# Two transformer layers on one core: the first attention item's operands copied chunk by chunk, and the zero rows copied before the second item's operands

## The reference, cut to what matters

```python
q = (x @ Wq + bq)...   # 16 heads of 16 values
k = (x @ Wk + bk)...   # 4 groups, each shared by 4 heads
v = (x @ Wv + bv)...
q_r = apply_rope(q / |q| * alpha * sqrt(16));  k_r = apply_rope(k / |k|)
attn = softmax(where(causal, q_r @ k_r.T / sqrt(16), -inf))
y = attn @ v;  x = layernorm(x + y @ Wo + bo)
```

## Time and profile before

| | |
|---|---|
| median of 3 runs | 808.29 us (807.83 to 812.68) |
| the profiled execution | 806.76 us |
| its span, first to last instruction | 805.1 us |
| busy, share of the span | TensorE 92%, VectorE 51%, ScalarE 49%, GpSimd 21% |
| mean granted TensorE clock | 0.952 of full |
| head of layer 0 | to about 88.6 us |
| first scores of layer 0 | 90.08 us |
| first scores of layer 1 | 383.01 us |

### The profile page before, as it was taken

How to read it: one execution, slowest core, us unless ns; L and a number is a source line. 1 busy time by engine, 2 the same in 40 slices (tenths; PEclk the granted TensorE clock), 3 DMA queues, 4 the chain that set the end, 5 groups by cost and what they waited for, 6 DMA issues and landing times.

```text
span 805.1 us, 10943 instructions
## 1 busy us (share of the span) xinstructions
PE 742.9 (92%) x3831; PEld 333.1 (41%) x3831; DVE 411.9 (51%) x998; ACT 394.4 (49%) x517; POOL 169.1 (21%) x185
## 2 busy tenths in 40 slices
PE   5999799999989899896999999989999999999996
PEld 1646222224322544342222222324466457448355
DVE  1579436334758788955043333365432842642524
ACT  1244688886868152553788888773121121130110
POOL 0012434343233123322143222331200200000000
PEclk9996599999999889999899999999999999999998
DMA  8401433332210000022444444470000000000000
GB/s 283 111 0 18 74 56 59 54 57 38 38 32 2 1 0 14 0 48 45 82 80 81 81 81 82 80 200 1 0 1 0 27 0 1 26 0 0 26 1 26
DMA packets 31601, 36.36 MB, mean 45 GB/s; under 512 B 7664, under 2 KB 19757, under 8 KB 31389
## 3 DMA queue, kind: packets, MB, share of 16 engines
q1 hardware_dynamic: 31541, 35.60, 21.8%
HBM read 12.74 MB, written 2.10 MB: 18 GB/s over the span
## 4 chain that ended last, share of the span: by engine, by line
PE 64%; DVE 15%; SPq 7%; ACT 6%; issue 4%; DMA 2%; POOL 1%; DVEq 0%; ACTq 0%; POOLq 0%
PE ps L1996 16%; PE ps L1255 13%; PE ps L1238 10%; PE ps L2020 9%; PE ps L1618 3%; SPq L972 3%; SPq L965 3%; ACT probs L1319 3%; PE ps L398 2%; DVE stats L289 1%; DVE raw L1155 1%; PE ps L643 1%; PE ps L667 1%; PE ps L1605 1%; PE ps L2006 1%
## 5 line engine op out<-in xcount | busy, mean ns | idle before, releaser
L1319 ACT ACTIVATE probs<-ps 128x1024 f32<-128x1024 f32 (+1 forms) x320 | 275.8, 965 | 66.2 <-PE ps L1238 65.9
L1238 PE MATMUL ps<-ops_mem 99*128 99x512 bf16 (+3 forms) x768 | 164.7, 336 | 14.6 <-issue 5.5
L1255 PE MATMUL ps<-probs,vstat 128*32 128x512 f32 (+3 forms) x1536 | 166.9, 507 | 11.4 <-DVE raw L1155 8.3
L1996 PE MATMUL ps<-ops_mem,parts_mem 128*128 128x512 f32 x320 | 147.2, 605 | 1.2 <-DVE probs L2048 1.2
L1335 POOL TENSOR_SCALAR_AFFINE_SELECT probs<-probs 128x512 f32<-128x512 f32 x128 | 85.0, 664 | 225.0 <-ACT probs L1319 224.3
L1238 PEld LDWEIGHTS ps<-ops_mem 99*128 99x128 bf16 x768 | 57.6, 99 | 164.2 <-ACT probs L1319 86.7
L1155 DVE COPY raw<-ps 128x512 f32<-128x512 f32 x32 | 22.1, 691 | 140.3 <-PE ps L1255 140.1
L1942 ACT ACTIVATE ops_mem<-ps 128x512 f32<-128x512 f32 x40 | 23.9, 597 | 142.7 <-PE ps L1996 139.9
L1996 PEld LDWEIGHTS ps<-ops_mem,parts_mem 128*128 128x128 f32 x320 | 58.9, 191 | 68.7 <-issue 66.0
L2020 PE MATMUL ps<-parts_mem,probs 128*128 128x256 f32 x320 | 70.5, 380 | 0.0
L2020 PEld LDWEIGHTS ps<-parts_mem,probs 128*128 128x128 f32 x320 | 60.3, 190 | 8.4 <-issue 0.5
(11 more groups left out here) (185 smaller groups left out, 729.7 us busy)
## 6 DMA issues: line engine op xcount, KB each, us to landing
ops_mem<-parts_mem SPq DMA_DIRECT2D x288, 64.0 KB
yT<-in_xT SPq DMA_DIRECT2D x4, 512.0 KB, 7.9
xres<-in_x SPq DMA_DIRECT2D x1, 2048.0 KB, 14.5
ops_mem<-parts_mem SPq DMA_DIRECT2D x48, 32.0 KB
out<-ops_mem SPq DMA_DIRECT2D x3, 512.0 KB, 3.0
rope<-in_rope SPq DMA_DIRECT2D x1, 1024.0 KB, 6.9
parts_mem<-in_wg SPq DMA_DIRECT2D x2, 512.0 KB, 4.8
parts_mem<-in_wu SPq DMA_DIRECT2D x2, 512.0 KB, 6.9
```

Of the source, the lines that this page charges most:

```text
L1238: last = nc.tensor.matmul(ps[:, bank, o:o + CH - lo], kT[0:KDIM, buf, h if kh == GH else 0, kt * P:(kt + 1) * P], qT[0:KDIM, buf, h, c * C ...
L1255: last = nc.tensor.matmul(ps[32 * h:32 * h + 32, AV, lo:CH], vstat[:, i % 2, kt, h if kh == GH else 0, :], probs[:, s % PRING, h, 0:CH - l ...
L1319: nc.scalar.activation(o, banks, ACT.Exp, scale=score_scale).then_inc(s_exp, 1)
L1996: last = nc.tensor.matmul(ps[:, 4 + 2 * (e % 2) + m, :], w, xT[:, kk, :], start=kk == 0, stop=kk == 1)
```

## The change

- Item 0's operands in layer 0 are copied in two halves by `stack_first`. The two constant rows go first, without a wait. Then come 18 DMAs for tokens 0 to 511, behind the low parts of chunk 0, and 18 for tokens 512 to 1023, behind those of chunk 1. TensorE waits for the first half and the constant rows (`early`) before step 0, and for the second half before step 4.
- For this the rotated tiles of the head leave the first operand buffer: `rot(u)` has 8 slots, all in the second buffer, and ScalarE waits before it uses one again.
- SyncE then issues the zeros of `no_shift`, behind waits for the head's projections and lengths (which use `yT`), and then item 1, behind a wait for the last `normalised`.
- The values of chunks 2 and 3 are copied raw out of PSUM by ScalarE (`keep_values`), and GpSimd adds their bias in eight additions behind item 0's fourth mask. VectorE's `values(2)` and `values(3)` go.
- VectorE's first copy of values stands ahead of its branch in both layers (`first_values`). The wait for the second sequence's values moves to item 4.

```diff
...
         s_v, s_bo = sem("s_v1"), sem("s_bo")
+        s_v0 = sem("s_v0")
         YN_COUNT, YN_HALF = 18, 11
...
             def rot(u):
-                b, j = u // (NU // 2), u % (NU // 2)
-                o = 2048 * b + 512 * j if j < 4 else 4096 + 2048 * b + 512 * (j - 4)
+                j = u % 8
+                o = 2048 + 512 * j if j < 4 else 6144 + 512 * (j - 4)
                 return ops_mem[:, o:o + 512]
...
                     act.wait_ge(s_rot, u + 1)
+                    if u >= 8:
+                        act.wait_ge(s_qn, u - 7)
                     nc.scalar.copy(rot(u), ps[:, R + u % 2, :]).then_inc(s_kept, 1)
...
                     nc.scalar.copy(part(u, 1), rest0[:, u % 4, :]).then_inc(s_mid, 1)
+                def keep_values(m):
+                    act.wait_ge(s_a, AT[m, NTL] + 1)
+                    nc.scalar.copy(vres[:, NG:2 * NG, m % 2 * CT:(m % 2 + 1) * CT, 0:HD].rearrange("p g t d -> p t g d"),
+                                   ps[:, A + AT[m, NTL] % 2, 0:CT * 64].rearrange("p (t g d) -> p t g d", t=CT, g=NG)
+                                   ).then_inc(s_v0, 1)
                 def keep_factors(m):
...
                 keep_hi(7)
+                keep_values(2)
                 keep_mid(6)
                 keep_hi(8)
+                keep_values(3)
                 keep_factors(3)
...
                 less_hi(7)
-                values(2)
-                values(3)
                 less_hi(8)
...
             def banks_free(pe):
-                pe.wait_ge(s_a_read, len(ORDER))
+                pe.wait_ge(s_a_read, len(ORDER) - 2)
+                pe.wait_ge(s_v0, 2)
                 pe.wait_ge(s_sq, NU)
...
                 yield
-            return banks_free
+            def rows_free(sp):
+                sp.wait_ge(s_a, len(ORDER))
+                sp.wait_ge(s_n2, NU)
+            def second_free(sp):
+                sp.wait_ge(s_qn, NU)
+            return banks_free, (rows_free, second_free)
         STEPS = [(c, kt) for c in range(2) for kt in range(4 * c + 4)]
...
                 self.s_shifted = sem(f"s_shifted{layer}")
+                if layer == 0:
+                    self.s_early = sem("s_early")
                 self.s_zero, self.s_decided = sem(f"s_zero{layer}"), sem(f"s_decided{layer}")
...
             def count(self, i):
+                if self.layer == 0 and i == 0:
+                    return 3 * NSLOT
                 return 2 * NSLOT + (NSLOT if self.layer == 0 else 2 * NSLOT) + (2 if i < 2 else GH)
+            def stack_first(self, sp):
+                s = self.s_stacked[0]
+                self.rows(sp, 0, self.s_early)
+                for m in range(2):
+                    toks = slice(m * CH, (m + 1) * CH)
+                    sp.wait_ge(s_parts[0], TILES[0] * (m + 1))
+                    for n in range(NSLOT):
+                        for j in range(2):
+                            sp.dma_start(qT[n * HD:n * HD + HD, 0, j::2, toks],
+                                         tq[HD * j:HD * j + HD, Q_PARTS[n], :, toks]
+                                         ).then_inc((self.s_early, s)[m], 16)
+                        sp.dma_start(kT[n * HD:n * HD + HD, 0, 0, toks], tk0[0:HD, K_PARTS[n], 0, toks]
+                                     ).then_inc((self.s_early, s)[m], 16)
+            def rows(self, sp, buf, s):
+                sp.dma_start(qT[ROWS:KDIM, buf, :, :], a["zeros"][:, 0:GH * T].rearrange("r (h n) -> r h n", h=GH)
+                             ).then_inc(s, 16)
+                sp.dma_start(kT[ROWS:KDIM, buf, :, :], a["ones"].rearrange("r (h n) -> r h n", h=GH)
+                             ).then_inc(s, 16)
             def stack(self, sp, i):
...
                 if i < 2:
-                    sp.dma_start(qT[ROWS:KDIM, buf, :, :], a["zeros"][:, 0:GH * T].rearrange("r (h n) -> r h n", h=GH)
-                                 ).then_inc(s, 16)
-                    sp.dma_start(kT[ROWS:KDIM, buf, :, :], a["ones"].rearrange("r (h n) -> r h n", h=GH)
-                                 ).then_inc(s, 16)
+                    self.rows(sp, buf, s)
                 else:
...
                 dve.wait_ge(self.s_stacked[i], 16 * self.count(i))
+                if i == 0 and self.layer == 0:
+                    self.early(dve)
                 for h in range(GH):
...
                 last.then_inc(self.s_shifted, 1)
+            def early(self, eng):
+                eng.wait_ge(self.s_early, 16 * (3 * NSLOT + 2))
             def there(self, pe, i):
...
             def fill(dve):
+                dve.wait_ge(s_parts[layer], TILES[layer] * NC)
                 vec = nc.vector
...
             kh = KEYS_OF[layer]
-            s_vstat = sem(f"s_vstat{layer}")
             s_scores = ops.s_scores
...
             def _(sp):
-                buffer_free(sp)
-                ops.stack(sp, 0)
-                sp.wait_ge(s_parts[layer], TILES[layer] * NC)
-                ops.stack(sp, 1)
-                ops.no_shift(sp)
+                if layer == 0:
+                    ops.stack_first(sp)
+                    rows_free, second_free = buffer_free
+                    rows_free(sp)
+                    ops.no_shift(sp)
+                    second_free(sp)
+                    ops.stack(sp, 1)
+                else:
+                    buffer_free(sp)
+                    ops.stack(sp, 0)
+                    sp.wait_ge(s_parts[1], TILES[1] * NC)
+                    ops.stack(sp, 1)
+                    ops.no_shift(sp)
                 sp.wait_ge(ops.s_zero, 16 * GH)
...
                     ops.stack(sp, i)
-            def values(dve, i):
-                buf = i % 2
-                nc.vector.tensor_copy(vstat[:, buf, :, 0:kh, HD * buf:HD * buf + HD],
-                                      vres[:, i, :, 0:kh * HD].rearrange("p t (n d) -> p t n d", d=HD)
-                                      ).then_inc(s_vstat, 1)
             def take(dve, i, c):
...
             def _(dve):
-                if layer == 1:
-                    dve.wait_ge(s_v, 2 * NC)
-                values(dve, 0)
                 for i in range(NI):
...
                     if i + 1 < NI:
-                        values(dve, i + 1)
+                        values(dve, layer, i + 1)
                     if i == 0:
...
                 next(free)
-                ops.there(pe, 0)
+                if layer == 0:
+                    ops.early(pe)
+                else:
+                    ops.there(pe, 0)
                 scores(0, 0)
...
                     more = i + 1 < NI
-                    pe.wait_ge(s_vstat, i + 1)
+                    pe.wait_ge(s_vstat[layer], i + 1)
                     for s in range(LAG, NS):
+                        if layer == 0 and i == 0 and s == 4:
+                            ops.there(pe, 0)
                         scores(i, s)
...
                         pool.wait_ge(s_y, NI)
-                        pool.wait_ge(s_vstat, NI // 2)
+                        pool.wait_ge(s_vstat[layer], NI // 2)
                         for g in range(NG // 2):
...
                         if layer == 0 and d == 3:
+                            if i == 0:
+                                pool.wait_ge(s_v0, 2)
+                                loaded(pool, "head")
+                                for t in range(TPB):
+                                    v = vres[:, NG:2 * NG, t, 0:HD]
+                                    last = nc.gpsimd.tensor_tensor(v, v, b_v[:, :].rearrange("p (g n) -> p g n", g=NG),
+                                                                   ALU.add)
+                                last.then_inc(s_v0, 1)
                             if i == 1:
...
                                 pool.wait_ge(s_y, NI)
-                                pool.wait_ge(s_vstat, NI // 2)
+                                pool.wait_ge(s_vstat[layer], NI // 2)
                                 ahead.stage(pool, 0)
...
                     end.apply(obuf).then_inc(s_o, 1)
-        banks_free = head()
+        banks_free, rooms_free = head()
         ops = [Operands(layer) for layer in range(2)]
+        s_vstat = [sem(f"s_vstat{layer}") for layer in range(2)]
+        def values(dve, layer, i):
+            buf, kh = i % 2, KEYS_OF[layer]
+            if i == NI // 2:
+                dve.wait_ge(*((s_v0, 3) if layer == 0 else (s_v, 2 * NC)))
+            nc.vector.tensor_copy(vstat[:, buf, :, 0:kh, HD * buf:HD * buf + HD],
+                                  vres[:, i, :, 0:kh * HD].rearrange("p t (n d) -> p t n d", d=HD)
+                                  ).then_inc(s_vstat[layer], 1)
+        def first_values(layer):
+            @on("vector")
+            def _(dve):
+                if layer == 1:
+                    dve.wait_ge(s_v, NC)
+                values(dve, layer, 0)
+        first_values(0)
         maxima(0, ops[0])
         ahead = Ahead()
-        last_item = attention(0, ops[0], None, banks_free, lambda sp: None, ahead=ahead)
```

(2 more changed lines are left out.)

## The result

The changed kernel has a median of 805.33 us (802.53 to 808.58 in 22 runs), the kernel before 808.14 us (803.19 to 812.94 in 22 runs beside them). The ratio is 0.9967, with a 95% interval of 0.9953 to 0.9982: 2.7 us faster, 1.5 to 3.8 us by the interval. That is within the 1% called the same.

A forecast was written before the change was run, and what follows sets the result against it. TensorE's 4.6 us wait before its first scores, mostly its branch, and VectorE's 11.2 us wait for zeros were the bounds aimed at; 0.95 + 1.28 - 0.15 = 2.1 us gained gave 806.2 us, range 803.5 to 809.3.

The forecast's parts named there:

- The sum and its two terms: Whole kernel: 0.95 us from earlier first scores plus 1.28 us from earlier zeros, less 0.15 us for the clock, 2.1 us.
- Start: Layer 0's first scores: they wait for no DMA, only TensorE's branch, and start at 89.1, 0.95 us earlier.
- I leave the branch where it was: TensorE's branch behind the head's last spread: its start unchanged, with -0.4 to +0.3 us kept for the range.
- ScalarE's copy at 0.4 us: Head, right ahead of the factor copy: an added 128x256 copy delays it 0.4 us, set against VectorE's freed 1.13 us.
- Zeros: Item 1's values product: with the zeros landed early it follows the mask, not item 0's late take, 1.28 us earlier.
- Clock: TensorE in item 0: if the rise from the lower clock level does not come forward, 0.4 us lost; 0.15 us taken.
- the forecast's price: Item 0 on TensorE at the lower clock level: 1.07 us lost over the 2.5 us from 94.25.
- It is what lets the start's gain through: VectorE's first copy of values, at 88.7 instead of 93.00: otherwise late for the earlier scores; adds no term.
- Rival A: Layer 0's start: the branch is no floor, scores at 85.5, 3.0 us gained, 4.3 with the zeros, 804.0 us; chance 0.10.
- Rival B: Layer 0: only the start's or only the zeros' part comes, 0.8 to 1.3 us gained, 807.2 us; chance 0.15.
- GpSimd's additions: Eight 128x64 additions behind item 0's fourth mask: 2.5 us from near 97.5, nothing on the path.
- Rival C: Between the layers: stretches at half clock grow or come again, making it slower, up to 809.6 us; chance 0.13.

The follow-up runs named there:

- the hoisted kernel: The changed kernel with layer 1's zeros ahead, ScalarE's last two middle casts later and TensorE's branch ahead of the head's last spreads; 802.83 us, ratio 0.9947 to before.

## Why the prediction was right, and where it was not

**The sum and its two terms.** 806.2 us was forecast, 805.33 us measured, inside the range. By matmul the lead of after over before was 1.81 us at the first scores and 115.85 - 113.42 = 2.43 us at item 1's product, against 2.1 us in the sum. Behind the mark it is 2.4 us in after and 3.1, 3.0 and 3.5 us in the other three executions with the same layer 0. So the waits and their order were right, and the sum was about 0.9 us too low, by the start. That the time came out within 0.9 us has luck in it, since single executions of either kernel lie 6 us and more apart.

**Start, 0.95 us forecast, 1.76 measured behind the mark.** What releases the scores was right: nothing but the branch, with 0.27 us behind it. The branch took 3.57 to 4.03 us in layer 0 in eleven profiled executions, whatever is copied ahead and wherever it is put. The Trainium skill (Runtime: NRT & Kernel Launch, section on instruction fetch mechanics) says that a taken branch to a page that isn't held forces a DMA fetch of that page before execution goes on. The traces agree: in all eleven the instruction queue (`q8 instruction` in the profile's table of DMA queues) moves one piece of 0.02 MB while the branch lasts and another within 4 us behind it, and none between 81 and 92 us in the two kernels without it. In after the first of the two moves between 85.0 and 85.5 us and in before between 86.5 and 88.9, and the branches last until 88.0 and 88.9; what fills the rest of them is not shown. Mis-sized was "I leave the branch where it was". The terms are: 1.16 us less 0.27 us that TensorE had waited beyond the end of the branch (0.89), 0.64 us because the branch starts earlier, and 0.23 us by which this execution's branch was shorter than the one of before (4.03), which is scatter, since unchanged code gave 3.58 us in the second run of after. The 0.64 us come from the eight additions taken from VectorE, as the kernel with the values back on VectorE shows (3.25 again). I had set them against ScalarE's copy at 0.4 us and called it even. The copy took 0.38 us in ScalarE's row, from 82.95, and the factor copy behind it starts at 83.21, 0.27 us later behind the mark than before's 83.00: that step was near. The other side was wrong. Before, the last spread waited for VectorE's subtraction behind the additions (84.04 + 0.69 = 84.73). In after that subtraction is done at 83.77, some 0.9 us earlier behind the mark, and the last spread follows the two before it without a wait, near 84.2. So 0.6 of VectorE's 1.13 us reached it, where ScalarE's copy had been expected to take them away.

**Zeros, 1.28 us forecast, 1.22 measured**, and 1.16 us when that part alone is undone. This step held in its mechanism as well: the take of item 0's second half was what came last, not the mask that the profile names.

**Clock, 0.15 us forecast, 0.6 us lost in this execution.** The windows of after (columns as in the earlier trace rows):

```profile
96.00:98.00 2.00, 2.00 (x17) 0.58 (x14) 0.00 (x0) 1.05 (x2) 2.00 (x7) 0.93 0.54 92
```

The granted clock of these two microseconds is 0.93 against 0.81 before, so the rise from 1.2 to 2.4 GHz came (0.93 - 0.81) x 2 / 0.5 = 0.48 us earlier, while TensorE's work came 1.8 us earlier. The lead fell from 90.08 - 88.27 = 1.81 us at the first scores to 110.94 - 109.72 = 1.22 us at item 1's. At the forecast's price (1.07 us per 2.5 us) the missing 1.81 - 0.48 us cost 0.57 us, and 0.59 us were lost.

The price holds, but the loss is this execution's and not the change's. In the four executions with the same layer 0 the rise, worked out from the means in the same way (granted clock 0.93 in 96 to 98 us, 0.79 and 0.90 in 94 to 96, 0.66 in 92 to 94) comes 8.0, 6.9, 6.2 and 5.7 us behind the first scores, and item 1's scores come 21.45, 20.96, 20.65 and 20.45 us behind them. That is 0.43 us for each us at the lower level, the forecast's price. Before has 6.7 and 20.86 us, in the middle. So against it the clock took between 0.6 us and -0.4 us, near nothing on average; the forecast's 0.15 us can't be told from that.

**"It is what lets the start's gain through"** (values ahead of VectorE's branch) was right in kind and too strong: without it 0.75 us of 1.8 us are lost, not all.

**Rival A** (the branch is no floor) fell: in after the scores wait until it is over. Its starts were right for the kernel without the branch: 85.5 us for the scores and 88.7 for step 1, against 85.27 and 88.57. But the product there leads before's by 12.61 - 10.47 = 2.1 us behind the mark and not by A's 3.0: ScalarE's casts stop it. **Rival B** (one part only) fell by the same table: both parts came. The zeros' part goes away with its own edit; of the start's part, 0.65 us go with the values and 0.27 us with the halves, and the rest was not undone by itself.

**GpSimd's additions** took 2.26 us for the eight, 2.5 us forecast, at 96.33, beside nothing on the path. Zeros at 86.8 to 90.0 came at 87.16 to 90.31, item 1's operands were in place with room, item 2's copying starts at 109.11, and item 2's product follows item 1's by 19.25 us (132.67 - 113.42), as forecast.

**Rival C, and why the profiled spans differ by 0.5 us.** I had written that a change of over 1 us in the distance from item 1 to the end would speak for C. It did change: from item 1's product to the end before took 805.1 - 115.85 = 689.2 us, after 804.6 - 113.42 = 691.2 us. What differs is where the lower-clock stretches lie. The first fence is before, the second after, the stretches around the end of layer 0's attention:

```profile
256.00:264.00 8.00, 4.89 (x50) 1.42 (x49) 7.93 (x12) 3.23 (x5) 5.14 (x5) 1.00 0.00 1
264.00:272.00 8.00, 6.90 (x22) 5.64 (x23) 7.69 (x14) 1.60 (x2) 0.00 (x0) 0.57 0.01 2
```

```profile
256.00:264.00 8.00, 4.34 (x40) 2.33 (x36) 7.86 (x15) 1.42 (x3) 3.81 (x4) 0.76 0.00 1
264.00:272.00 8.00, 7.44 (x21) 6.04 (x22) 7.76 (x10) 1.68 (x3) 0.00 (x0) 0.60 0.01 2
```

After falls to the lower level four microseconds earlier and comes out of it at nearly the same moment, and by 282 us its lead of 2.4 is down to 1.5 us. In the other stretch, 288 to 296, after has the better clock, 0.82 against 0.58. Such gains and losses follow to the end. That this is the execution and not the change is seen where the code behind item 1 is the same: from item 1's product to the end the second run of after took 806.4 - 112.6 = 693.8 us, the kernel with the values on VectorE 801.0 - 114.6 = 686.4 us, that without a branch 806.7 - 112.7 = 694.0 us, and five more lie between them (689.7 to 691.1). So C is real as scatter of some 8 us between executions, with before inside it, and the medians show no systematic loss: they are 2.7 us apart by the ratio, against leads of 2.4 to 3.5 us at item 1's product. Whether the change shifts these stretches by a few tenths on average was not separated; the interval of the ratio is too wide for it.

## What to carry to other kernels

When an engine's wait is put down to a DMA, look at that engine's own sequencer rows beside it: 3.5 of the 4.6 us here were a jump, and what paid was to start the jump earlier or to put it where the engine waits anyway. Before pricing the removal of a floor, find the next one on every engine that takes part (here ScalarE's two casts), since it decides what is left. An order in a DMA queue is worth reading for small pieces that many wait for: four small DMAs ahead of twenty large ones gave 1.2 us in layer 0, and took most of 1.4 to 3.1 us of waiting out of layer 1. And before an execution's loss is put down to the change, read the same distance in other executions of the same code: here the clock's rise alone moved it by 1.0 us.

## What the runs showed of the hardware that I had not expected

The jump over a part that is not entered cost TensorE 3.57 to 4.21 us in all 24 cases (both layers, 13 profiled executions), whatever was copied beside it, with one piece of the instruction queue moving in each of layer 0's eleven; in the hoisted kernel layer 0's cost nothing, since TensorE had to wait past its end anyway.

Executions of the same kernel spread over 6 to 7 us (802.5 to 808.6 for after in the first set, 803.3 to 810.6 in the second), and the two profiled ones, 806.34 and 808.09 us, had mean granted clocks of 0.954 and 0.948. A step of a few tenths of a microsecond in the program can't be seen in one time of it, but it can in the distance to a mark: item 1's distance is 3.69 us in all eleven executions that have the zeros ahead, and the branch starts 2.51 to 2.61 us behind the mark in all eight that keep the values on ScalarE and the branch in its place.
